# Routing and experts in one block, and the two sweeps of a mixture-of-experts layer as one stream of steps

## The reference

```python
logits = x @ router_w + router_b                 # x: (4096, 128), 64 experts
probs = softmax(logits)
top_w, top_idx = top_k(probs, 42)                # 42 of 64 experts
top_w = softmax(top_w)
comb = zeros((N, 64)).at[..., top_idx].set(top_w)
h = gelu(einsum('td,edh->teh', xt, w1) + b1)     # hidden 256
y = einsum('teh,ehd->ted', h, w2) + b2
out = einsum('ted,te->td', y, comb)              # added to the residual h
```

## Time and profile before

| what | value |
|---|---|
| median of 3 runs | 1970.97 us (1968.58 to 1971.7) |
| the profiled execution, its own time | 1968.94 us |
| its span | 1967.2 us |
| mean granted TensorE clock | 0.954 of 2.4 GHz |
| busy share of the span | PE 92%, DVE 90%, ACT 74%, POOL 37% |
| routing | about 484 to 549 us |
| experts, sweep 0 and sweep 1 | from 550 and 1258 us |

### The profile page before, as it was taken

How to read it: one execution, slowest core, us unless ns; L and a number is a source line. 1 busy time by engine, 2 the same in 40 slices (tenths; PEclk the granted TensorE clock), 3 DMA queues, 4 the chain that set the end, 5 groups by cost and what they waited for, 6 DMA issues and landing times.

```text
span 1967.2 us, 28778 instructions
## 1 busy us (share of the span) xinstructions
PE 1805.4 (92%) x8438; PEld 1439.0 (73%) x8438; DVE 1778.7 (90%) x2271; ACT 1458.1 (74%) x2616; POOL 722.3 (37%) x471
## 2 busy tenths in 40 slices
PE   6467669997689999999999999999999999999998
PEld 4344446665468888888888888788888888888887
DVE  8558878884979999999999999899999999999997
ACT  2144557886868888888888888788888888888886
POOL 4255356663223333333333333233333333333330
PEclk9967779999589999999999999999999999999999
DMA  7500000000133333333333332233333333333331
GB/s 217 147 27 16 1 1 1 0 0 22 62 113 129 114 126 118 122 120 120 127 113 127 113 132 108 107 111 129 114 126 117 123 122 118 124 116 128 111 124 47
DMA packets 105256, 191.45 MB, mean 97 GB/s; under 512 B 13558, under 2 KB 86246, under 8 KB 88550
## 3 DMA queue, kind: packets, MB, share of 16 engines
q1 hardware_dynamic: 103166, 186.77, 27.1%
q0 software_dynamic: 2048, 4.20, 0.7%
HBM read 179.40 MB, written 11.53 MB: 97 GB/s over the span
## 4 chain that ended last, share of the span: by engine, by line
PE 71%; DVE 0%; issue 0%; POOL 0%; ACT 0%; DVEq 0%; ACTq 0%; POOLq 0%
PE f_ps_h L1916 12%; PE f_ps_h L1918 12%; PE f_ps_h L1917 12%; PE f_ps_y L1927 12%; PE f_ps_y L1929 12%; PE f_ps_y L1928 12%; PE f_ps_y L1943 0%; DVE s_lo L1872 0%; DVE scaled L1866 0%; PE f_ps_h L1954 0%; ACT act_out L1826 0%; POOL w_lo L1730 0%; DVEq L1746 0%; POOL w_hi L1728 0%; PE f_ps_h L1898 0%
## 5 line engine op out<-in xcount | busy, mean ns | idle before, releaser
L1826 ACT ACTIVATE act_out<-f_ps_h,b_t 128x512 f32<-128x512 f32 x1024 | 649.7, 686 | 265.7 <-PE f_ps_h L1918 265.6
L1866 DVE TENSOR_TENSOR scaled<-act_out,c_row 128x1024 f32<-128x1024 f32 x512 | 753.1, 1471 | 41.2 <-ACT act_out L1826 40.6
L1872 DVE TENSOR_TENSOR s_lo<-scaled,s_hi 128x1024 fp32r<-128x1024 f32 x512 | 672.8, 1314 | 0.1
L1834 ACT ACTIVATE s_hi<-scaled 128x1024 fp32r<-128x1024 f32 x512 | 542.1, 1059 | 2.0 <-DVE scaled L1866 1.5
L1728 POOL CAST w_hi<-w_raw 128x512 fp32r<-128x512 f32 x128 | 200.7, 1568 | 909.6 <-PE f_ps_y L1929 895.8
L1927 PE MATMUL f_ps_y<-s_hi,w_hi 128*128 128x512 f32 x1024 | 398.7, 389 | 3.0 <-DVE s_lo L1872 3.0
L1916 PE MATMUL f_ps_h<-x_hi,w_hi 128*128 x1024 | 399.8, 390 | 1.1 <-DVE b_t L1856 0.6
L1917 PE MATMUL f_ps_h<-x_lo,w_hi 128*128 x1024 | 399.1, 390 | 0.0
L1918 PE MATMUL f_ps_h<-x_hi,w_lo 128*128 x1024 | 399.1, 390 | 0.0
L1929 PE MATMUL f_ps_y<-s_hi,w_lo 128*128 128x512 f32 x1024 | 398.4, 389 | 0.0
L1928 PE MATMUL f_ps_y<-s_lo,w_hi 128*128 128x512 f32 x1024 | 398.4, 389 | 0.0
(11 more groups left out here) (220 smaller groups left out, 1575.3 us busy)
## 6 DMA issues: line engine op xcount, KB each, us to landing
c_row<-comb_rows SPq DMA_DIRECT2D x128, 1024.0 KB, 4.7
w_raw<-in_w SPq DMA_DIRECT2D x256, 128.0 KB, 4.1
by_slot<-b_zeros SPq DMA_DIRECT2D x1, 3072.0 KB, 13.3
b_gauss_s<-by_slot SPq DMA_DIRECT2D x12, 256.0 KB, 5.6
mixed_rows<-mixed SPq DMA_DIRECT2D x12, 256.0 KB, 2.2
out<-h SPq DMA_DIRECT2D x8, 256.0 KB, 4.6
cent<-in_centers SPq DMA_DIRECT2D x1, 1536.0 KB
neg_prec<-in_logvar SPq DMA_DIRECT2D x1, 1536.0 KB
```

The costliest lines, as they stand in the source:

```text
L1826: last = act.activation(act_out[:, r % 2, c, :], ps_h[:, r % 2, c, :], ACT.Gelu, bias=b1_t[:, c, bass.ds(e, 1)])
L1834: act.activation(s_hi[:, r % RING], scaled[:, r % RING], ACT.Copy).then_inc(hi_ready, 1)
L1866: dve.tensor_tensor(scaled[:, r % RING], act_out[:, r % 2], c_row[:, k, g * GT:(g + 1) * GT].unsqueeze(1).broadcast_to([P, HC, GT]), ALU.m ...
L1872: dve.tensor_tensor(s_lo[:, r % RING], scaled[:, r % RING], s_hi[:, r % RING].bitcast(F32), ALU.subtract).then_inc(lo_ready, 1)
```

## The change

Three things are changed.

1. Routing and experts share one block, so that no engine waits for all others between them. The last quad's `weigh`, `copy_comb` and `turn_comb` leave the routing loop and are called in the first steps of the experts (ACT and PE, step 1), and the bias matmuls of sweep 0 move from after step 1 to after step 3. b1 is turned in the routing, into a bank of `r_ps_c`, and DVE copies it there.
2. The sweep loop is written out. Sweep 1 begins without emptying the pipeline: its steps 0 to 3 contain the last 4 `second` of sweep 0.
3. The sums of sweep 0 are copied, turned, added and restarted group by group within steps 1 to 5 of sweep 1: ACT copies group r - 1 in step r (1 to 4), PE turns it in step r, now into the group's own bank of `f_ps_y`, DVE adds group r - 2 in step r (2 to 5), and PE waits for that add and writes the bias term, also in step r.

```diff
@@ route, tensor engine
             turn_x(1)
             logit(1)
-            for s in range(QUADS + 1):
+            pe.wait_ge(f["b1_in"], 16)
+            for c in range(HC):
+                last = pe.transpose(ps_c[:, 1, c * EXPERTS:(c + 1) * EXPERTS], f["b1_rows"][:, c * P:(c + 1) * P],
+                                    ident[0:EXPERTS, 0:EXPERTS])
+            last.then_inc(b1_turned, 1)
+            for s in range(QUADS):
                 turn_x(s + 2)
                 logit(s + 2)
-                turn_comb(s - 1)
+                if s == 2:
+                    pe.wait_ge(b1_copied, 1)
+                turn_comb(pe, s - 1)
@@ route, vector engine
             maximum(0)
             probabilities(0)
+            dve.wait_ge(b1_turned, 1)
+            dve.tensor_copy(b1_t[:], ps_c[:, 1, 0:HC * EXPERTS].rearrange("p (c e) -> p c e", c=HC)
+                            ).then_inc(b1_copied, 1)
@@ experts, scalar engine
-            act.wait_ge(y_added, GROUPS)
-            with act.Fori(0, SWEEPS) as w:
+            def copy_y(w, g):
+                act.wait_ge(summed, w * STEPS + (STEPS - GROUPS + g + 1))
+                act.activation(y_t[:, g, :], ps_y[:, g, :], ACT.Copy).then_inc(y_copied, 1)
...
+            act.wait_ge(b1_copied, 1)
+            for w in range(SWEEPS):
                 start = w * STEPS
                 for r in range(BODY):
                     gelu(start + r, r // GROUPS, r)
-                    if r:
-                        high(start + (r - 1), r - 1, r - 1 >= LAG)
+                    if w == 0 and r == 1:
+                        last_weights(act)
+                    if w or r:
+                        high(start + (r - 1), (r - 1) % BODY, w > 0 or r - 1 >= LAG)
+                    if w == 0 and r == 1:
+                        last_comb(act)
+                    if w and 1 <= r <= GROUPS:
+                        copy_y(w - 1, r - 1)
@@ experts, vector engine
+            def add_y(w, g):
+                dve.wait_ge(y_turned, w * GROUPS + (g + 1))
...
+            for w in range(SWEEPS):
                 for r in range(BODY):
-                    scale(start + r, rows + 16, r, r >= RING)
-                    if r:
-                        low(start + (r - 1), r - 1)
+                    scale(start + r, rows + 16, r, w > 0 or r >= RING)
+                    if w or r:
+                        low(start + (r - 1), (r - 1) % BODY)
+                    if w and 2 <= r < 2 + GROUPS:
+                        add_y(w - 1, r - 2)
@@ experts, tensor engine
+            def turn_y(w, g):
+                pe.wait_ge(y_copied, w * GROUPS + (g + 1))
+                for t in range(GTILES):
+                    last = pe.transpose(ps_y[:, g, t * P:(t + 1) * P], y_t[:, g, t * P:(t + 1) * P], ident[:])
+                last.then_inc(y_turned, 1)
...
                 for r in range(BODY):
-                    if r < 2:
-                        pe.wait_ge(y_added, w * GROUPS + (GROUPS - HC + r * HC))
                     if r >= LAG:
                         second(start + (r - LAG), r - LAG, False)
-                    first(start + r, w * EXPERTS + r // GROUPS, w, r, r >= 2)
-                    if r == 1:
+                    elif w:
+                        second(start - LAG + r, BODY - LAG + r, True)
+                    first(start + r, w * EXPERTS + r // GROUPS, w, r, w > 0 or r >= 2)
+                    if w == 0 and r == 1:
+                        last_turn(pe)
+                    if w == 0 and r == LAG - 1:
+                        pe.wait_ge(b2_in, 16)
+                        pe.wait_ge(comb_copied, QUADS_OF_ROUTE)
                         for g in range(GROUPS):
-                            pe.matmul(ps_y[:, g, :], b2_rows[:], comb_t[:, tokens(w, g)], start=True, stop=False)
+                            bias_y(w, g)
+                    if w and 1 <= r <= GROUPS:
+                        turn_y(w - 1, r - 1)
+                    if w and 2 <= r < 2 + GROUPS:
+                        pe.wait_ge(y_added, (w - 1) * GROUPS + (r - 1))
+                        bias_y(w, r - 2)
```

More of the change, by code:

```diff
@@ L1468, in spread, with weigh, copy_comb, turn_comb @@
             return of_tile.unsqueeze(2).broadcast_to([P, QT, EXPERTS])
+        def weigh(act, q):
+            if in_range(q, QUADS):
+                b = q % 2
+                act.wait_ge(r2_ready, q + 1)
+                after(act, comb_turned, q - 1)
+                for k in range(QT):
+                    last = act.activation(comb[:, b, k, :], top[:, b, k, :], ACT.Copy, scale=r2[:, b, k:k + 1])
+                last.then_inc(comb_ready, 1)
+        def copy_comb(act, q):
+            if in_range(q, QUADS):
+                act.wait_ge(comb_turned, q + 1)
+                act.activation(comb_t[:, cols(q)], ps_c[0:EXPERTS, q % 2], ACT.Copy).then_inc(comb_copied, 1)
+        def turn_comb(pe, q):
+            if in_range(q, QUADS):
+                after(pe, comb_copied, q - 1)
+                pe.wait_ge(comb_ready, q + 1)
+                for k in range(QT):
+                    last = pe.transpose(ps_c[0:EXPERTS, q % 2, k * P:(k + 1) * P], comb[:, q % 2, k, :], ident[:])
+                last.then_inc(comb_turned, 1)
         @block.sync
@@ L1529, in second_exps @@
                     last.then_inc(exp_two, 1)
[L1531 to L1543, removed]
             norm(0)
@@ L1730, in split_weights, with experts @@
     pool.tensor_tensor(w_lo[:, r], w_raw[:, r], w_hi[:, r].bitcast(F32), ALU.subtract).then_inc(f["w_split"], 1)
-def experts(nc, h, ident, x_hi, x_lo, comb_t, f, loader, out):
+def experts(nc, block, signals, h, ident, x_hi, x_lo, comb_t, f, loader, b1_t, act_out, scaled, routed, out):
     LAG = 4
@@ L1847, in _ @@
                         high(start + i * BODY + (r - 1), (r - 1) % BODY, True)
[L1848 to L1851, removed]
+            high(SWEEPS * STEPS - 1, BODY - 1, True)
+            for g in range(GROUPS):
+                copy_y(SWEEPS - 1, g)
         @block.vector
         def _(dve):
-            dve.wait_ge(b1_turned, 1)
-            dve.tensor_copy(b1_t[:], ps_h[:, 0, 0, 0:HC * EXPERTS].rearrange("p (c e) -> p c e", c=HC)
-                            ).then_inc(y_added, GROUPS)
             def scale(S, rows_loaded, r, reuse):
@@ L1948, in _ @@
                         first(at + r, w * EXPERTS + i * WRING + r // GROUPS, w, r, True)
-                for r in range(LAG):
-                    second(start + (STEPS - LAG + r), BODY - LAG + r, True)
-                for g in range(GROUPS):
-                    pe.wait_ge(y_copied, w * GROUPS + (g + 1))
-                    for t in range(GTILES):
-                        last = pe.transpose(ps_h[:, g // HC, g % HC, t * P:(t + 1) * P],
-                                            y_t[:, g, t * P:(t + 1) * P], ident[:])
-                    last.then_inc(y_turned, 1)
+            for r in range(LAG):
+                second(SWEEPS * STEPS - LAG + r, BODY - LAG + r, True)
+            for g in range(GROUPS):
+                turn_y(SWEEPS - 1, g)
 _OUTS = [((BATCH, SEQ, DIM), "float32")]
```

85 lines of the change are left out of this document (44 added, 41 removed).

## The result

| | before | after |
|---|---|---|
| median of 4 runs, same chip | 1969.78 us (1966.31 to 1971.70) | 1993.57 us (1989.39 to 1996.59) |
| ratio, 95% interval | | 1.0121 (1.0095 to 1.0147) |
| profiled execution, span | 1968.94, 1967.2 us | 1991.61, 1989.9 us |
| mean granted clock | 0.954 | 0.948 |

The changed kernel is 1.2% slower; 1995 was forecast. The page shows the busy times of the earlier trace rows again, in a span that is 22.7 us longer. First the busy line, then the granted clock in 40 slices; its last 7 is the slice with the turn of the sweeps.

The account below looks back on a forecast made before the run. PE's own matmuls were taken to bound the kernel. PE idle time at the turn +16.8, clock +9 and start with routing -1.1 gave +24.7 us, 1993.6 to 1995.7; forecast 1995, 8-in-10 range 1983 to 2002.

Parts of the forecast that it names:

- likeliest case: Whole kernel: PE idles at the turn of the sweeps and its clock drops; 1995 us, spanning 1990 to 2001; chance 0.68.
- (a): Turn of the sweeps: same PE idle time, but the clock holds; +15.7 us, about 1985.5; chance 0.2.
- (b): Turn of the sweeps: ACT copies each sum before PE reaches its transposes; -4.6 us, about 1965; chance 0.05.
- (c): Turn of the sweeps: PE waits in the first step only; -1.5 us, no change that can be told; chance 0.02.
- (d): Longer PE program slows each step, or half clock lasts from first gap to last; +37 us, about 2007; chance 0.05.
- Waits: Turn of the sweeps: PE idles for ACT's copies and DVE's adds, 20.3 us against 3.5 before; +16.8 us.
- Clock: Turn of the sweeps: 4.5 PE bursts behind gaps lose 2.0 us each at half clock; +9 us, bounds 0 and 11.5.
- Routing to experts: Last reciprocal to first `second`: barrier gone, but the last `weigh` stands behind two gelus; -2.3 us, bounds -4.1 and -1.6.
- Into the routing: Work moved into the routing: b1's transposes and copy +0.9 us, POOL's moved work +0.3.
- The splits: POOL's splits of experts 2 and 3 run during the routing and slow DVE; +0.3 us, bounds 0 and 0.7.
- The table load: ACT's 1.28 us load moves ahead of its wait for PE's first expert matmuls; costs nothing, 1.3 us if late.
- the end of sweep 1: Kernel's end: as before except for the bank into which PE turns; costs nothing.

Follow-up runs that it names:

- two moved lines away: Changed kernel with ACT's copy moved ahead of the step's gelu and DVE's add ahead of its scale; ratio 0.9980 to the kernel before.
- the filled kernel: Changed kernel with its turn waits kept, but PE fills them with matmuls on a zero matrix; ratio 1.0096 to the kernel before.
- 32 gaps of 3.3 us: Kernel with copy and add moved ahead, plus a PE wait for DVE's scale behind step 8 of every 16; ratio 1.0885 to the kernel before.
- 32 of 1.5: Kernel with copy and add moved ahead, plus a PE wait for ACT's gelu behind step 8 of every 16; ratio 1.0276 to the kernel before.
- the second lone gap: Kernel with copy and add moved ahead, plus one PE wait for DVE's scale in step 8 of each sweep, here sweep 1's; ratio 1.0037 to the kernel before.

## Why the prediction was right

**Forecast and rivals.** The time, the sign and the likeliest case held. Rival (a), clock unharmed, fell with the granted clock of 0.70 to 0.80 at the turn; (b) and (c), no lasting waits, with the eight idle times; (d) with steady steps at 1299, where clock and rhythm are those of the earlier trace rows. (b) is nonetheless a kernel that exists: two moved lines away, at 0.9980.

**Waits, +16.8 forecast, 17.6 measured** (T of the filled kernel against before). The chain was right in kind and number. From the slot of the last `first` to the transposes pass 2.95 us each time, in after and in the filled kernel (3.1 forecast; the bracket's 2.79 counts from the modelled end); behind the transposes 1.21 to 1.25 in the filled kernel (1.1 forecast), and 0.5 to 1.0 in after, where two of the three groups of transposes ran at half clock; before the last bias 4.59 (4.6 forecast). At full clock that is 20.1 of the 20.3 forecast, and less the 3.5 of before 16.6. The other 1.0 was left out of the forecast: the interleaved order costs PE changes between kinds of matmul, with the last wait some 2 us once nothing else waits. That the brackets of after also add up to 17.6 is chance: nothing of before is subtracted there.

**Clock, +9 forecast, 8.9 measured.** The forecast was four and a half bursts at 2.0; five at 1.5 to 2.2 were found. That the two agree to 0.1 is luck; the size of a burst and their number were each off by a tenth. Some 24 us at half clock lose 12, and 3 of these were hidden in waits. The choice near the upper bound, since every gap was longer than any that had left the clock whole, was the right one: 32 gaps of 3.3 us cost 2.0 each, 32 of 1.5 nothing. The rule of the Trainium skill (TensorE: Matmul & The Clock Gate, Part 1) that "the default state is throttled, and activity releases the throttle" would have given 10; it fits the long gaps, but taken literally not the short ones, the second lone gap, nor the 2.39 us that cost the clock in some traces and not in others.

**Routing to experts, -2.3 forecast, -4.1 measured,** at the bound; the other seven traces with this start give -3.2 to -5.7, two of them beyond it. The step that was mis-sized is "at half clock 5.1 us, until 549.0": the clock was whole from 546.5, PE ended `first(1)` at 547.9, and the last scaling began at 549.28 instead of 550.5. The transposes followed at 550.48. In the eight traces six to ten of the first twelve matmuls ran at half clock, never all. That half of the room is taken by the weights behind two gelus was right, and moving them gave 3.6 us against this trace.

**Into the routing, +1.2 forecast, +1.5 measured.** b1 was put at 0.9 and cost 0.6 (from the first to the second `r_neg_max` 4.90 us instead of 4.29). The splits were put at 0.3 with 0.7 as upper bound and cost 1.1: the prediction looked at `neg_p`, which took 1.16 beside a split, and not at `top`, which took 1.52 instead of 0.5. That bound failed; it was too small a term to matter.

The table load cost nothing, the end of sweep 1 neither: from ACT's last `gelu` (1954.1, then 1977.0) to the end pass 13.1 and 12.9 us.

The net was right partly by cancelling: the start was 1.8 better than forecast, the turn 0.7 worse, and 1.2 us of the untouched part are chance.

## What to carry to other kernels

To drain a pipeline costs only its idle time; to stream through the seam costs whatever stands in front of each hand-over in program order. When work is woven into a loop, put each hand-over on the receiving engine ahead of the instruction that waits for the current step, on every engine of the chain at once: of 27 us the copy moved alone gave 3 and the add alone 9. Price a new wait on PE with the clock behind it: here an idle 2.8 to 3.3 us cost about two more in all cases but two, 2.4 us did so in some traces and not in others, 1.5 us never.

## What had not been expected of the hardware

- The clock behind equal gaps is not equal. Of the 34 long gaps 33 were followed by 3 to 4 or by some 6 us at half clock, and one by none; nor did the first gap of 2.79 us in the run with the add moved cost anything, where the same gap in after did. What decides between them stays open.
- A change between kinds of matmul costs PE 0.1 us at full clock (0.34 instead of 0.227 to the next start), which ate up 1.4 of the 3.5 us that streaming was to save. The same 0.34 stands behind each of the short gaps, where the kind does not change.
- One DVE instruction that takes 0.5 us elsewhere took 1.52 beside POOL's subtraction of two weight tiles, and another, `neg_p`, 1.16 instead of 0.42 beside an earlier one; the instructions right beside them kept their length.
- Code that nobody touched took 483 to 494 us from one trace to the next, partly with the chip. A stretch between two marks in the traces told 0.2 us apart where the medians told 2.
